# Splitting the K rows of three cross-attentions on GpSimd from an fp32 copy, with a four-slot ring of probabilities and an earlier fetch of the context

## The chip, the cores and the metric

The kernel runs on one NeuronCore of a Trainium2 chip. Its engines work side by side, each through its own instruction stream: TensorE (PE), VectorE (DVE), ScalarE (ACT), GpSimd (POOL) and SyncE (SP), which here issues nearly all DMAs. They wait for each other by semaphores. The metric is the device time of one execution in microseconds (us).

## The reference

A chain of four blocks updates x, of shape 16 batches x 56 tokens x 128. Block 0 attends from x to a context of 1500 rows per batch with one head of width 128, and sends the result through a router with three experts. Blocks 1, 2 and 3 each hold one cross-attention of 16 heads of width 8 to the same context of 1500 rows; blocks 2 and 3 also hold a self-attention over the 56 tokens and an MLP. The cross-attention, as block 1 has it:

```python
xq = _ada_ln(x_q, t_vec, Wss_q, bss_q)
xkv = _ada_ln(x_kv, t_vec, Wss_kv, bss_kv)
q = (xq @ Wq + bq).reshape(B, Lq, nh, dh)          # B=16, Lq=56, nh=16, dh=8
kv = (xkv @ Wkv + bkv).reshape(B, Lkv, 2, nh, dh)  # Lkv=1500
k = kv[:, :, 0]
v = kv[:, :, 1]
scores = jnp.einsum('bqhd,bkhd->bhqk', q, k) / jnp.sqrt(jnp.float32(dh))
attn = jax.nn.softmax(scores, axis=-1)
out = jnp.einsum('bhqk,bkhd->bqhd', attn, v).reshape(B, Lq, H)
return x_q + (out @ Wp + bp)
```

Block 2 normalises the context without modulation, block 3 takes it as it is.

## The kernel before, in words

The queries and keys of a cross-attention are carried as sums of two fp16 numbers, a high part (`k_hi`) and a low part (`k_lo`, what is left of the fp32 value). The score matmuls contract over 50 rows: 2 rows that carry the row maximum, then high and low parts of 16 dims stacked as rows. To get the parts of K into these rows, each third of a batch's keys (500 columns, t = 0, 1, 2) is written to DRAM (`k_out`, two DMAs, L407) and read back six times into `k_st` (`k_in`, six DMAs, L419). SP issues both, in a fixed order.

A cross-attention loops over the 16 batches (`pipeline`: two batches ahead of the loop, ten in it, four behind it). One pass, `attend(batch, following, behind, third)`, runs through 12 slots c, one for each chunk of 125 keys. In a slot PE computes the scores of `batch` (`scores`, L1153), two or three tiles that find the row maxima of the following batch (`unit`, L1101, 24 per batch, in a ring of three PSUM banks), in odd slots the product of probabilities and values for two earlier chunks (`values`, L1127), and one step of the preparation of the batch after that, `behind`. The table `SLOT_MISC` puts the nine steps in slots: T0, T1, T2 (transposes of the context, L1011) in slots 1 to 3, K0, K1, K2 (the K projection, L1016) in slots 4, 6 and 8, V0, V1 (L1022) in slots 9 and 10, and V2 in slot 0 of the next pass. All nine share one PSUM bank, so each step waits until the one before it has been read out.

ACT takes exponentials of the scores into a ring of six buffers (`probs`, `RING`, L795) and reads the steps out: for K it writes `k_hi` in fp16 (L725). DVE finds the maxima (L1552) and computes `k_lo` from the same PSUM bank and `k_hi` (`k_low`, L1460), behind the maxima of the slot after the step. PE's next step waits on both semaphores:

```python
if was == "K":
    pe.wait_ge(sem("k_hi_done"), NT * n + wt + 1)
    pe.wait_ge(sem("k_lo_done"), NT * n + wt + 1)
```

At the end of a pass a short chain joins the engines: DVE turns the maxima into two fp16 parts (L1564 to L1566), PE moves them to rows (L1112), DVE and ACT write them beside the queries (L1574, L782).

POOL normalises the context of batch b+3 in blocks 1 and 2 (`normalise`, 12 instructions, L585) and has nothing to do in the loop of block 3. SP issues, in each pass, the third K part of `following`, the queries (`q_st`, `q_mx`, L454), then `k_out` and `k_in` of `behind`, and last the load of the context of batch b+4 (L373), which waits until T2 of `behind` is done.

The first 17 of the preparation steps of a block (all of batch 0, all but V2 of batch 1) run earlier, beside the experts of block 0 or beside the first eight batches of a self-attention (`AHEAD`, `ahead`). In a self-attention POOL makes three copies for each batch (`self_copies`, L544 to L548).

## Time and profile before

| | |
|---|---|
| median of three runs | 2054.87 us (2048.06 to 2065.39) |
| the profiled execution | 2056.51 us, of which the span of the trace is 2054.7 us |
| busy share of the span | PE 80%, weight loads 50%, DVE 60%, ACT 49%, POOL 21% |
| mean granted TensorE clock | 0.892 of full speed |
| loops of the cross-attentions | about 410 to 800, 1005 to 1395 and 1610 to 2000 us |
| DMA | 166 MB, 81 GB/s over the span |

The busy shares are averages over stages with different limits. A busy PE also counts time in which matmuls overlap in its pipeline. In the chain of work that ended last, "issue" is time in which the engine waited for nothing that the profile shows.

### The profile page before, as it was taken

Reading aid. Unit: us, or ns where it says so; the run is one execution under the profiler, and the core shown is the slowest. Engines: PE = TensorE matmul, PEld = TensorE weight load, DVE = VectorE, ACT = ScalarE, POOL = GpSimd, SP = SyncE. Lnnn points to the kernel's source line nnn. Section 1 sums busy time; section 2 is a strip of 40 time slices with the busy share of each in tenths; the row PEclk is TensorE's granted clock in tenths of the full one; section 3 lists DMA queues with packets and bytes.
Section 4 is the critical chain, followed back from the end, with each engine's and each line's share of the span. In section 5 each row is a group of like instructions: output and inputs, shape, how many; then the busy total and the mean of one; then the engine's idle time right before and its main releaser. Section 6 shows DMA issues by size and latency. Waiting matters only on the chain.

```text
span 2054.7 us, 53923 instructions
## 1 busy us (share of the span) xinstructions
PE 1635.4 (80%) x20495; PEld 1030.7 (50%) x20495; DVE 1236.0 (60%) x2433; ACT 1004.1 (49%) x1911; POOL 422.9 (21%) x611
## 2 busy tenths in 40 slices
PE   4788777588887887787688888887785888888876
PEld 3465544255555555443355555555342455555554
DVE  5454443567775776364677777773364777777762
ACT  1243322166665666242366666663242466666662
POOL 7000133013331333135033333310131000000000
PEclk9798988599998998796699999996796799999997
DMA  5021122234443442040344444430040444444410
GB/s 174 26 77 64 45 44 62 55 82 112 112 110 94 113 102 73 1 103 3 72 112 113 111 109 111 110 98 14 0 102 11 92 116 117 114 114 112 106 43 9
DMA packets 178537, 166.32 MB, mean 81 GB/s; under 512 B 67551, under 2 KB 168098, under 8 KB 178402
## 3 DMA queue, kind: packets, MB, share of 16 engines
q1 hardware_dynamic: 176818, 163.35, 30.2%
q8 instruction: 97, 1.59, 0.4%
q10 hardware_dynamic: 1008, 1.05, 0.2%
q14 instruction: 38, 0.31, 0.0%
q0 software_dynamic: 576, 0.02, 0.0%
HBM read 114.46 MB, written 40.08 MB: 75 GB/s over the span
## 4 chain that ended last, share of the span: by engine, by line
PE 64%; issue 13%; DVE 10%; ACT 10%; DMA 1%; POOL 1%; ACTq 0%; DVEq 0%; SPq 0%; POOLq 0%
PE PS L1127 11%; PE PS L1022 8%; PE PS L1153 8%; PE PS L1016 8%; PE PS L862 6%; PE PS L1101 5%; PE PS L1011 3%; PE PS L941 3%; ACT q_parts L795 2%; DVE mx L1552 2%; PE PS L1227 2%; PE PS L959 2%; ACT v_sb L729 2%; ACT cxT L720 2%; PE PS L932 1%
## 5 line engine op out<-in xcount | busy, mean ns | idle before, releaser
L1552 DVE TENSOR_REDUCE mx<-PS 112x1 f32<-112x500 f32 x1152 | 718.4, 671 | 295.8 <-PE PS L1101 291.5
L795 ACT ACTIVATE q_parts<-PS 125x448 f32<-125x448 f32 x1152 | 562.2, 544 | 108.8 <-PE PS L1153 105.0
L585 POOL TENSOR_SCALAR cx<-cx,norm_b 125x128 f32<-125x128 f32 x384 | 303.5, 813 | 590.7 <-DMA cx<-in_ctx 488.2
L1153 PE MATMUL PS<-q_st,k_st 50*125 50x112 f16 x4608 | 263.1, 236 | 40.1 <-ACT q_parts L795 23.2
L1153 PEld LDWEIGHTS PS<-q_st,k_st 50*125 50x125 f16 x4608 | 186.4, 140 | 213.7 <-ACT q_parts L795 121.7
L1101 PE MATMUL PS<-k_st,q_mx 50*112 50x500 f16 x1152 | 262.5, 403 | 38.8 <-issue 24.2
L1127 PE MATMUL PS<-q_parts,v_sb 125*18 125x112 f32 x9216 | 291.4, 270 | 0.0
L1127 PEld LDWEIGHTS PS<-q_parts,v_sb 125*18 125x18 f32 x9216 | 218.4, 101 | 60.7 <-issue 52.1
L729 ACT ACTIVATE v_sb<-PS 125x512 f32<-125x512 f32 x144 | 87.1, 605 | 186.7 <-PE PS L1022 186.6
L725 ACT ACTIVATE k_hi<-PS,vec 128x500 f16<-128x500 f32 x144 | 97.5, 677 | 129.0 <-PE PS L1016 129.0
L1101 PEld LDWEIGHTS PS<-k_st,q_mx 50*112 50x112 f16 x1152 | 91.5, 133 | 74.5 <-issue 44.9
L1460 DVE SCALAR_TENSOR_TENSOR k_lo<-PS,vec,k_hi 128x500 f16<-128x500 f32 x144 | 104.8, 728 | 20.0 <-ACT k_hi L725 20.0
L1011 PE MATMUL PS<-ident,cx 125*128 125x125 f32 x576 | 97.1, 293 | 22.6 <-ACT cxT L717 11.8
L1011 PEld LDWEIGHTS PS<-ident,cx 125*128 125x128 f32 x576 | 62.6, 146 | 63.4 <-issue 26.3
L1022 PE MATMUL PS<-L_xcond_Wkv,cxT 128*125 128x128 f32 x384 | 61.1, 308 | 27.3 <-issue 22.6
L1022 PE MATMUL PS<-L_xcond_W_kvc,cxT 128*125 128x128 f32 x384 | 61.1, 308 | 25.0 <-issue 22.9
L1016 PE MATMUL PS<-cxT,L_xcond_Wkv 128*128 128x500 f32 x96 | 54.7, 653 | 30.8 <-issue 25.9
L813 ACT ACTIVATE A<-A 56x896 f32<-56x896 f32 x32 | 30.4, 949 | 92.4 <-DVE A L1661 92.4
L1022 PE MATMUL PS<-L_xcond_ca_vw,cxT 128*125 128x128 f32 x384 | 55.2, 287 | 25.3 <-issue 22.9
L782 ACT ACTIVATE q_st<-PS 2x448 f16<-2x448 f32 x48 | 25.7, 535 | 101.4 <-PE PS L1112 100.0
L1392 DVE TENSOR_REDUCE neg<-PS 56x1 f32<-56x1500 f32 x16 | 27.4, 1711 | 77.1 <-PE PS L941 77.1
L1022 PEld LDWEIGHTS PS<-L_xcond_Wkv,cxT 128*125 128x125 f32 x384 | 52.2, 209 | 42.2 <-issue 36.5
(266 smaller groups left out, 1994.1 us busy)
## 6 DMA issues: line engine op xcount, KB each, us to landing
k_st<-k_dram SPq DMA_DIRECT2D x864, 62.5 KB, 2.2
cx<-in_ctx SPq DMA_DIRECT2D x56, 750.0 KB
k_dram<-k_hi SPq DMA_DIRECT2D x144, 125.0 KB, 1.8
k_dram<-k_lo SPq DMA_DIRECT2D x144, 125.0 KB, 2.0
v_sb<-in_ctx SPq DMA_DIRECT2D x8, 750.0 KB
q_mx<-q_all SPq DMA_DIRECT2D x48, 99.8 KB
q_st<-q_all SPq DMA_DIRECT2D x48, 99.8 KB
q_all<-q_dram SPq DMA_DIRECT2D x18, 196.0 KB, 6.4
```

What stands on the lines that cost most here:

```text
L585: last = pool.tensor_scalar(cx[:, p, c, :], cx[:, p, c, :], norm_b[:, p, 0, c:c + 1], norm_b[:, p, 1, c:c + 1], ALU.subtract, ALU.mult)
L729: act.activation(v_sb[:, p, TC * t:TC * t + TC, :, 0:2 * DH], PS[0:KC, bank, :].rearrange("p (c r d) -> p c r d", c=TC, r=NP), ACT.Copy)\
L795: act.activation(probs[:, c % RING, u * HR:(u + 1) * HR], PS[0:KC, (2 * c + u) % SC_RING, 0:HR], ACT.Exp).then_inc(sem("exp_done"), 1)
L862: last = mm(dst[:, u, :], wt, r(u), start=(k == 0), stop=(k == len(rows) - 1))
L1011: last = pe.transpose(PS[:, bank, c * KC:(c + 1) * KC], cx[:, p, TC * t + c, :], ident[0:KC, 0:KC])
L1016: mm(PS[:, bank, 0:TK], cr["kw"], cxT[:, TK * t:TK * t + TK], start=True, stop=True)\
L1022: last = mm(PS[0:KC, bank, c * D:(c + 1) * D], cxT[:, k0:k0 + KC], cr["vw"], start=True, stop=True)
L1101: mm(PS[0:PW, MX_BANK + u % MX_RING, 0:TK], q_mx[64 * a:64 * a + ROWS, p, k, :], k_st[64 * a:64 * a + ROWS, p, k, TK * t:TK * t + TK], sta ...
L1127: last = mm(PS[32 * j:32 * j + VW, PV_BANK, k * PW:k * PW + PW], v_sb[:, p, c, r, :], probs[:, c % RING, r * PW:r * PW + PW], start=(c == ...
L1153: last = mm(PS[0:KC, (2 * c + a) % SC_RING, k * PW:k * PW + PW], k_st[64 * a:64 * a + ROWS, p, k, c * KC:(c + 1) * KC], q_st[64 * a:64 * a ...
L1460: dve.scalar_tensor_tensor(out=k_lo[:, cols], in0=PS[:, bank, 0:TK], scalar=cr["kb"], in1=k_hi[:, cols], op0=ALU.add, op1=ALU.subtract)\
L1552: dve.tensor_reduce(mx[:, r, t:t + 1], PS[0:PW, MX_BANK + u % MX_RING, 0:TK], AX.X, ALU.max)\
```

## The change

Four things change, and the work that is computed stays the same.

1. ACT writes the whole K tile in fp32 into a new buffer, `k_full` (two batches deep). POOL makes `k_hi` from it by a cast and `k_lo` by a subtraction (`split_keys`). DVE's `k_low` is gone everywhere.
2. PE's next step waits for ACT's copy alone (`k_full_done`).
3. The ring of probabilities has four buffers in place of six.
4. SP issues the load of batch b+4 ahead of the K parts of `behind`.

POOL's split of the first two batches of a block (`split_first`) stands behind `self_copies` of the whole self-attention.

```diff
--- before.py
+++ after.py
@@ -31,7 +31,7 @@
 QUAD = 4
 ROWS = 2 + 3 * 2 * DH
 VW = 2 * DH + 2
-RING = 6
+RING = 4
 UNITS = NP * NT
 
 
@@ -180,6 +180,7 @@
         mod_b = sb("mod_b", [128, 2, 2])
 
 
+        k_full = sb("k_full", [128, 2, S])
         k_hi = sb("k_hi", [128, S], F16)
         k_lo = sb("k_lo", [128, S], F16)
         k_st = sb("k_st", [128, 2, QUAD, S], F16)
@@ -481,13 +482,13 @@
                         q_scores(following)
                     if behind:
                         q_max(behind)
+                        if not (isinstance(b, int) and b + 4 >= B):
+                            load((b + 4, i + 2, p))
                         k_out(behind, 0)
                         k_in(behind, 0)
                         k_out(behind, 1)
                         k_in(behind, 1)
                         k_out(behind, 2)
-                        if not (isinstance(b, int) and b + 4 >= B):
-                            load((b + 4, i + 2, p))
 
                 pipeline(sp, first, attend)
 
@@ -557,6 +558,22 @@
                     for p in range(2):
                         copies((2 * i + p, i, p))
 
+            def split_keys(layer, batch, t):
+
+                b, i, p = batch
+                n = B * (layer - 1) + b
+                cols = slice(TK * t, TK * t + TK)
+                ge_known(pool, ("k_full_done", NT * n + t + 1), (f"k_out{t}", 32 * n))
+                pool.tensor_copy(k_hi[:, cols], k_full[:, p, cols]).then_inc(sem("k_hi_done"), 1)
+                ge_known(pool, ("k_hi_done", NT * n + t + 1))
+                pool.tensor_tensor(k_lo[:, cols], k_full[:, p, cols], k_hi[:, cols], ALU.subtract)\
+                    .then_inc(sem("k_lo_done"), 1)
+
+            def split_first(layer):
+                for b in range(2):
+                    for t in range(NT):
+                        split_keys(layer, (b, 0, b), t)
+
             def cross_copies(layer, rest):
                 cr = cross_of(layer)
                 n0 = B * cr["n"]
@@ -600,6 +617,9 @@
                     if third and cr["norm"] is not None:
                         copies(third)
                         normalise(third)
+                    if behind:
+                        for t in range(NT):
+                            split_keys(layer, behind, t)
 
                 def first():
                     if cr["norm"] is not None:
@@ -614,13 +634,16 @@
                 pool.wait_ge(sem("bn_done"), B)
                 for p in range(2):
                     pool.memset(v_sb[:, p, :, :, 2 * DH:VW], 1.0).then_inc(sem("v_ones"), 1)
+                split_first(1)
                 cross_copies(1, True)
             if layers > 2:
                 cross_copies(2, False)
                 self_copies(2)
+                split_first(2)
                 cross_copies(2, True)
             if layers > 3:
                 self_copies(3)
+                split_first(3)
                 cross_copies(3, True)
 
 
@@ -721,9 +744,9 @@
                     elif kind == "K":
                         act.wait_ge(sem("k_ready"), NT * n + t + 1)
 
-                        ge(act, f"k_out{t}", 32 * n)
-                        act.activation(k_hi[:, TK * t:TK * t + TK], PS[:, bank, 0:TK], ACT.Identity, bias=cr["kb"])\
-                           .then_inc(sem("k_hi_done"), 1)
+                        ge(act, "k_lo_done", NT * (n - 2) + t + 1)
+                        act.activation(k_full[:, p, TK * t:TK * t + TK], PS[:, bank, 0:TK], ACT.Identity, bias=cr["kb"])\
+                           .then_inc(sem("k_full_done"), 1)
                     else:
                         act.wait_ge(sem("v_ready"), NT * n + t + 1)
                         act.activation(v_sb[:, p, TC * t:TC * t + TC, :, 0:2 * DH],
@@ -997,8 +1020,7 @@
                     else:
                         was, wt = MISC[k - 1]
                         if was == "K":
-                            pe.wait_ge(sem("k_hi_done"), NT * n + wt + 1)
-                            pe.wait_ge(sem("k_lo_done"), NT * n + wt + 1)
+                            pe.wait_ge(sem("k_full_done"), NT * n + wt + 1)
                         else:
                             ge(pe, {"T": "cxT_done", "V": "v_done"}[was], NT * n + wt + 1)
                     if kind == "T":
@@ -1443,33 +1465,12 @@
                 l0_recip(b)
                 l0_evidence(b)
 
-            def preparation(layer):
-
-                cr = cross_of(layer)
-                n0 = B * cr["n"]
-
-                def k_low(batch, k, bank=MISC_BANK):
-                    kind, t = MISC[k]
-                    if kind != "K":
-                        return
-                    b, i, p = batch
-                    n = n0 + b
-                    dve.wait_ge(sem("k_hi_done"), NT * n + t + 1)
-                    ge(dve, f"k_out{t}", 32 * n)
-                    cols = slice(TK * t, TK * t + TK)
-                    dve.scalar_tensor_tensor(out=k_lo[:, cols], in0=PS[:, bank, 0:TK], scalar=cr["kb"],
-                                             in1=k_hi[:, cols], op0=ALU.add, op1=ALU.subtract)\
-                       .then_inc(sem("k_lo_done"), 1)
-
-                return k_low
-
             l0_batches(l0_first, l0_both, l0_last, dve)
             for k in range(2):
                 dve.wait_ge(sem("std_done"), k + 1)
                 dve.reciprocal(rstd_all[:, k, :, :], std_all[:, :, :]).then_inc(sem("rstd_done"), 1)
             dve.wait_ge(sem("evid_ready"), 1)
             dve.tensor_copy(halves(A[5]), pair(0)).then_inc(sem("evid_done"), 1)
-            k_low = preparation(1)
 
             for e in range(E):
                 dve.wait_ge(sem("router_ready"), e + 1)
...
@@ -1614,9 +1609,6 @@
                             finish((b - 1, None, 1 - p))
                         for t in tiles:
                             unit(following, t)
-                        of_next, k = SLOT_MISC.get(c - 1, (True, None))
-                        if behind and not of_next:
-                            k_low(behind, k)
                     if following:
                         shift_split(following)
                     if p == 0 and not start:
...
```

SP, one pass in the loop of block 1, before (DMA rows by out<-in; L454 are the queries, L407 and L419 the K parts, L373 the context of batch b+4):

```order
L454 DMA q_mx<-q_all 114x4x112
L278 ISA
L407 DMA k_dram<-k_hi 128x500
L407 DMA k_dram<-k_lo 128x500
...
L222 REGISTER_ALU
L373 ISA
L373 DMA cx<-in_ctx 125x1536
L278 REGISTER_ALU
L419 DMA k_st<-k_dram 16x4x500 x6
```

The same place in the changed kernel (its lines are one further down):

```order
L455 DMA q_mx<-q_all 114x4x112
L223 ISA
L374 ISA
L374 DMA cx<-in_ctx 125x1536
L279 ISA
L408 DMA k_dram<-k_hi 128x500
L408 DMA k_dram<-k_lo 128x500
L279 ISA
L420 DMA k_st<-k_dram 16x4x500 x6
```

The context load moved ahead of all three pairs of K writes of its pass, and ahead of the first two groups of six K reads; the third group stands at the start of the next pass in both.

POOL, one pass in the loop of block 1, in the changed kernel (before, the rows of L567 and L569 and the two L279 between them were not there):

```order
L586 COPY norm_b<-mean_all 125x12
L588 REGISTER_ALU
L588 COPY norm_b<-rstd_all 125x12
L223 REGISTER_ALU
L594 ISA
L594 COPY mod_b<-mod 128x2
L279 ISA
L602 TENSOR_SCALAR cx<-cx,norm_b 125x128 x12
L279 ISA
L567 CAST k_hi<-k_full 128x500
L569 TENSOR_TENSOR k_lo<-k_full,k_hi 128x500
...
```

The split of three tiles of `behind` follows the normalising of the batch after it, in POOL's own order.

DVE around K0 in the loop of block 1, before:

```order
L1552 TENSOR_REDUCE mx<-PS 112x1
L1457 ISA
L222 REGISTER_ALU
L1460 SCALAR_TENSOR_TENSOR k_lo<-PS,vec,k_hi 128x500
L1551 REGISTER_ALU
L1552 TENSOR_REDUCE mx<-PS 112x1
```

In the changed kernel the maxima follow each other without it, and nothing else moved on DVE.

## Rows read from the trace of the kernel before

**Rows 1.** The page, part 4: the chain that ended last, shares by engine.
```profile
PE 64%; issue 13%; DVE 10%; ACT 10%; DMA 1%; POOL 1%; ACTq 0%; DVEq 0%; SPq 0%; POOLq 0%
```

**Rows 2.** That chain in order of time, 500 to 560 us: start, us, what.
```profile
501.19 0.57 issue
...
505.19 0.86 issue
...
508.81 1.53 issue
```

**Rows 3.** The timeline, 500 to 545 us, all engines: start, us, engine, line, operation, out<-in.
```profile
500.94 0.73 DVE L1460 SCALAR_TENSOR_TENSOR k_lo<-PS,vec,k_hi 128x500 f16<-128x500 f32 x1
501.76 1.08 PE L1016 MATMUL PS<-cxT,L_xcond_Wkv 128*128 128x500 f32 x2 [0.57 <-issue]
...
502.88 0.68 ACT L725 ACTIVATE k_hi<-PS,vec 128x500 f16<-128x500 f32 x1 [0.89 <-PE PS L1016]
...
509.51 0.73 DVE L1460 SCALAR_TENSOR_TENSOR k_lo<-PS,vec,k_hi 128x500 f16<-128x500 f32 x1
...
515.35 0.31 SPq L373 DMA_DIRECT2D cx<-in_ctx  x1
...
526.14 0.68 ACT L725 ACTIVATE k_hi<-PS,vec 128x500 f16<-128x500 f32 x1 [0.41 <-PE PS L1016]
```

**Rows 4.** PE's waits in block 1's loop, 420 to 790 us: total us, times, longest.
```profile
PE PS L1022 <- issue: 22.6, 15, 1.5
PE PS L1016 <- issue: 20.0, 28, 0.9
```

**Rows 5.** The waits of the whole trace, same columns.
```profile
PE PS L1016 <- issue: 72.0, 91, 3.0
...
PE PS L1022 <- issue: 68.4, 45, 1.5
```

**Rows 6.** The page, part 5: busy us, mean ns; idle before, releaser.
```profile
L1552 DVE TENSOR_REDUCE mx<-PS 112x1 f32<-112x500 f32 x1152 | 718.4, 671 | 295.8 <-PE PS L1101 291.5
...
L1460 DVE SCALAR_TENSOR_TENSOR k_lo<-PS,vec,k_hi 128x500 f16<-128x500 f32 x144 | 104.8, 728 | 20.0 <-ACT k_hi L725 20.0
```

**Rows 7.** Busy us by engine in stretches: PE, PEld, DVE, ACT, POOL; clock, DMA share, GB/s.
```profile
517.10:543.67 26.57, 22.45 (x370) 15.05 (x371) 19.48 (x35) 17.31 (x34) 9.74 (x15) 1.00 0.44 113
...
1726.18:1752.38 26.20, 22.58 (x370) 15.05 (x371) 19.57 (x36) 16.67 (x35) 0.00 (x0) 1.00 0.44 113
```

**Rows 8.** POOL's groups by form: busy us, mean ns.
```profile
L548 POOL TENSOR_TENSOR q_parts<-A,mask 128x896 f32<-128x896 f32 x32 | 54.1, 1689 | 0.0
...
L545 POOL COPY A_first<-A 128x112 f32 x28 | 7.9, 282 | 0.0
L544 POOL COPY A_first<-A 128x56 f32 x28 | 6.5, 231 | 95.5 <-PE PS L1227 95.5
```

**Rows 9.** SP's timeline in block 3's loop, 1705 to 1765 us.
```profile
1726.18 0.35 SPq L407 DMA_DIRECT2D k_dram<-k_hi  x1
...
1728.76 2.66 SPq L419 DMA_DIRECT2D k_st<-k_dram  x6
...
1738.09 0.31 SPq L373 DMA_DIRECT2D cx<-in_ctx  x1
...
1743.32 3.02 SPq L454 DMA_DIRECT2D q_mx<-q_all  x1
```

**Rows 10.** POOL's timeline, 300 to 1700 us.
```profile
526.04 9.35 POOL L585 TENSOR_SCALAR cx<-cx,norm_b 125x128 f32<-125x128 f32 x12 [18.09 <-DMA cx<-in_ctx]
...
1555.44 1.69 POOL L548 TENSOR_TENSOR q_parts<-A,mask 128x896 f32<-128x896 f32 x1
```

**Rows 11.** SP's timeline between self- and cross-attention of block 3, 1380 to 1640 us.
```profile
1528.43 8.93 SPq L419 DMA_DIRECT2D k_st<-k_dram  x18
1584.04 0.81 SPq L441 DMA_DIRECT2D q_dram<-q_parts  x2
```

**Rows 12.** Line 1566: duration in ns min/median/max, first and last start.
```profile
L1566 DVE SCALAR_TENSOR_TENSOR msplit<-mneg,msplit x48: 170/171/341, 408.3 to 1987.9; 112x8 f16<-112x8 f32 x48
```

More of the change, by code:

```diff
@@ L1493, in _ @@
             for k in range(2 * E + 1):
-                if layers > 1:
-                    ahead(k_low, AHEAD[3 * k:3 * k + 1], DENSE_BANK)
                 dve.wait_ge(sem("hid_tanh"), k + 1)
@@ L1502, in _ @@
                                          op0=ALU.add, op1=ALU.mult).then_inc(sem("hid_done"), 1)
-                if layers > 1:
-                    ahead(k_low, AHEAD[3 * k + 1:3 * k + 3], DENSE_BANK)
                 if k == 1:
@@ L1544, in cross @@
                     last.then_inc(sem("q_split"), 1)
-                k_low = preparation(layer)
                 def unit(batch, u):
@@ L1641, in self_attention @@
                 s, _, bs, _, ob = SELF[layer]
-                k_low = preparation(layer)
                 dve.wait_ge(sem("self_lin"), 2 * s + 1)
@@ L1675, in both @@
                     front(n)
-                    ahead(k_low, beside[0:1], SELF_BANK)
                     back(b)
-                    ahead(k_low, beside[1:3], SELF_BANK)
                 batches(dve, front, both, back)
```

## The prediction, written before the changed kernel was timed

> **What bounds the kernel now.** I read the chain that ended last first. PE holds 64% of it, and 13% is "issue", time without a releaser in the profile [rows 1]. In order of time, most of this in the loops is three gaps per pass: 0.57 us ahead of K1, 0.86 us ahead of K2, 1.53 us ahead of V0 [rows 2]. Then the timeline: DVE's subtraction for K0 starts at 500.94 and takes 0.73, so it ends at 501.67; PE's K1 starts at 501.76, 0.09 later. For K2 it ends at 510.24 and V0 starts at 510.34, 0.1 later [rows 2, 3]. ACT's copy of K1 was over by 503.56, while PE was still in the scores and maxima of its slot [rows 3]. So these gaps are PE's wait for `k_lo`: DVE is free to take it up only behind the maxima of the next slot. They total 2.96 us a pass. Rows 4 repeat this over one loop: 20.0 us in 28 gaps (14 passes, two each) and about 1.5 us each ahead of V0. DVE itself is not the bound. It is busy 19.5 of 26.2 to 26.6 us per pass, ACT 16.7 to 17.3, POOL 9.7, PE 22.5 [rows 7]. It is the order on DVE that costs.
>
> **The change part by part.**
>
> *PE's waits in the loops.* `behind` exists in 14 passes of each of three blocks, 42 in all. 42 x 2.96 = 124.3 us. ACT's K copy (0.68 us) starts 0.04 us after the projection ends and precedes ACT's exponentials of the slot, so it is over before PE wants the bank in slots 4 to 9. Does something else wait there at once? I moved the pass of rows 3 up by the gaps. DVE then has the 8 tiles of slots 7 to 9 in about 5.0 us of PE's work; at 671 ns each [rows 6] that is 5.4 us, less where they follow each other, with 2.2 us of subtractions gone (728 ns x 3 [rows 6]). The three-bank ring lets DVE lag by three tiles, and V0, 1.1 us without a maximum, lets it catch up. ACT has 17.3 us of work in a pass of then 23.6 [rows 7]. I take the whole 124.3; the bounds are none of it (0) and all.
>
> *The steps ahead of the loops.* Beside the dense stage and the self-attentions the projection follows more closely. Of the whole trace's 91 and 45 gaps, 84 and 42 lie in loops; 7 and 3 remain, with 72.0 - 60.0 = 12 us and 68.4 - 42 x 1.53 = 4 us [rows 4, 5]. ACT's copy stays in these, DVE's 0.73 + 0.09 goes: 10 x 0.82 = 8 us at most, 0 if the softmax chain of these stages hides it. I take 5.
>
> *POOL's two instructions per tile.* The trace has no cast or subtraction of 500 elements on POOL. Copies of 56 and 112 elements take 231 and 282 ns, 0.91 ns an element, so 0.64 us for 500 (fp16 output, no row: up to the 0.73 of DVE and more). The two-input one takes 1689 ns for 896 [rows 8]: 0.94 us by proportion, 1.69 us at most. So 1.6 to 2.7 us a tile with semaphores 1.9, 5.7 us a pass. With the normalising (9.74 [rows 7]) POOL is at 15.4 of 23.6 us in blocks 1 and 2, at 5.7 in block 3. Its split of `behind` stands behind the normalising of the next batch, and that behind the context load. That load is now issued at slot 3 of the pass before and lands some 10.7 us later at worst (515.35 to POOL's start at 526.04 [rows 3, 10]). POOL then starts normalising when it has split K2, at about 18 us of a pass, and ends 9.35 us later [rows 10], some 4.5 us into the next; K0's copy ends 9.7 us into a pass (526.82, of the pass that starts at 517.10 [rows 3, 7]). Covered, with 5 us to spare. Without the earlier load the normalising would end about when K0 is ready.
>
> *SP.* The number of DMAs stays. SP's chain of a pass runs from `k_out` of K0 through three landings and three groups of reads to the end of `q_mx`: 1726.18 to 1746.34, 20.2 us with the load inside [rows 9]. K0's parts leave 1.1 us later than before (1.9 against 0.73 plus waiting for the maxima, which about evens out). The load goes some 4.5 us ahead of them: T2 is one slot before K0's projection, which starts 1.1 us ahead of ACT's copy at 526.14 [rows 3], and the parts are there at 528.7. SP has been idle in that time. The pass shrinks to 23.2, so SP has 3.0 us left. The reads of K0 are issued by 16.9 us of a pass (9.7 + 1.9, then 2.58 to the first read and 2.66 for the six [rows 9]) and are wanted at its end, those of K1 and K2 only at units 8 and 16 of the next. I take 0.
>
> *Ring of four.* ACT waits for the values of chunk c-4 ahead of chunk c. In PE's order they stand ahead of the scores of chunk c in every slot, the first ones of a pass too, and ACT needs those scores anyway. 0 us; nothing covers it, it cannot end last.
>
> *Between the stages.* The K parts of batches 0 and 1 used to leave during the self-attention; now six tiles are split behind POOL's last copy. In block 3 this copy ends at 1557.13 [rows 10]. Three tiles (5.7) and a pair of writes (0.8), load (0.3), 18 reads (8.9 [rows 11]), three pairs of writes (2.3), load (0.3), 18 reads (8.9): 1584.3. SP should write the queries at 1584.04 [rows 11], so it is just late, later if reads wait for their writes, and the queries share the DMA engines with what is in flight: 0 to +6, I take +3. In block 2 the norm lies between, which makes it 0.
>
> *The shared port.* The last of the three small DVE operations that split the maxima reads two SBUF operands: 171 ns typically, 341 ns once [rows 12]. POOL now works nearly always in blocks 1 and 2, so it may more often have to wait for one instruction, up to 0.78 us for one of the twelve of the normalising (9.35 / 12 [rows 10]). 28 passes x 0 to 0.78 is 0 to 22 us; the median of 171 beside a POOL busy for a third of the pass is nearer to nothing, and I take 3.
> The Trainium skill (SBUF — State Buffer, Who interferes with whom) says that DVE and GpSimd share one pair of ports under an exclusive lock, that a DVE instruction with two SBUF inputs is fully blocked by a reading GpSimd instruction, and that a tensor_reduce is never. By it the sum would hold these 3 us and up to 22; were the rule void it would be 3 us lower. The single 341 ns agrees; nothing in this trace settles it.
>
> *Sum.* 2056.5 - 124.3 - 5 + 3 + 3 = 1933 us against the profiled execution, which lies 1.6 us above the median.
>
> **The rivals.**
>
> *Another engine takes the gaps (maxima or exponentials).* If DVE's maxima still lag where PE now comes sooner, half of the V0 gap returns: 0.8 x 42 = 34 us, 1967. For: DVE's 5.4 against PE's 5.0 us above. Against: the rest of its pass is loose, 17.3 of 23.6 us.
>
> *The load pushes the K rows.* If K0's writes land only with the whole load, 10.7 us after its issue, they land 6.2 us after theirs in place of 2: SP's chain becomes 24.4 us and sets the pass. 1.2 x 42 = 50 us of the gain are lost: 1984. Against: 10.7 us was with six reads and the queries just behind the load [rows 3, 9], which are now not there.
> The Trainium skill (DMA: Bandwidth & Descriptors, Queues, rings and completion order) says that descriptors of one ring are consumed in order on each DMA engine, so writes issued behind a load queue behind its bytes. By it this rival, not the forecast, would hold if the load were that long; no row shows the load alone.
>
> *Slower.* The same mechanism at more than one landing. SP has 6.0 us up to the old 26.2 us pass; from there on every pass is longer than before. Two landings late by 4.2 us each give 28.6 us, 2.4 x 42 = 101 us more: 2157. For it: `q_mx` takes SP 3.02 us to issue when a load and six reads are in flight [rows 9]. Against: by K1 the load has had over 9 us.
>
> *It does not do what it says.* If the gaps were the sequencer's own time and the 0.1 us a coincidence, only DVE is relieved: about 2050, within 1%. Against: it would be the same coincidence each time.
>
> **How the numbers follow.** Forecast 0.62 (1905 to 1955), another engine takes part 0.15 (1955 to 1975), the load pushes the K rows 0.12 (1975 to 2000), no effect 0.05, slower 0.03, better than 1905 0.03 (more overlap than I count). The time is that of the likeliest: 1933 us. The range 1905 to 1985 takes the first two and half of the third, about 0.83. One per cent, about 20 us, is what a measurement of this kernel tells from nothing. Faster by over 1%: 0.62 + 0.15 + 0.12 + 0.03 = 0.92; within 0.04; slower 0.04.
>
> **What would show it.** In the profile after: no gap of 0.57, 0.86 and 1.53 us ahead of K1, K2 and V0, and a pass of about 23.2 us; waits of PE for maxima (first rival) or of PE for `k_st` reads or queries, with SP without idle time (second and third); POOL's cast and subtraction at 1.6 to 2.7 us a tile; SP's first query write in block 3 directly behind the last K reads. The prediction is wrong if POOL needs over 3.5 us a tile, since its pass would then exceed 20 us and K2's parts would be late, or if the pass stays above 25 us with the gaps gone.

## The result, and the profile after

| kernel | median | runs | lowest to highest |
|---|---|---|---|
| before | 2059.76 us | 4 | 2048.06 to 2065.39 |
| changed | 1986.99 us | 4 | 1983.16 to 1990.89 |

The changed kernel takes 0.9654 of the time before (95% interval 0.96 to 0.9708). That is 73 us faster, where 122 were forecast (1933 against the 2054.87 known then), and 2 us outside the range. The profiled execution took 1983.74 us with a span of 1981.9, against 2054.7 before.

The chain that ended last comes first again. These are its shares by engine and by line, on the page of the changed kernel:

```profile
PE 44%; DMA 16%; SPq 10%; issue 9%; DVE 9%; ACT 6%; POOL 6%; DVEq 0%; POOLq 0%; ACTq 0%
```

PE held 64% of it before, and DMA 1% [rows 1]. Now DMA and SP's queue hold 26% together. In order of time, 1739 to 1771 us, in block 3's loop (start, us, what):

```profile
1739.40 6.39 DMA k_dram<-k_lo
...
1749.10 1.87 DMA k_dram<-k_lo
...
1754.26 1.95 DMA k_dram<-k_lo
...
1762.43 8.15 DMA k_dram<-k_lo
```

The chain runs through SP from one write of K parts to the next. The waits for K0 are 6.4 and 8.2 us long, those for K1 and K2 1.9 and 2.0: the write that stands behind the context load is the long one. SP's own timeline shows where the load is (1690 to 1765 us of the changed kernel; start, us, queue, line, what):

```profile
1712.08 0.38 SPq L374 DMA_DIRECT2D cx<-in_ctx  x1
1715.94 0.35 SPq L408 DMA_DIRECT2D k_dram<-k_hi  x1
...
1721.31 2.68 SPq L420 DMA_DIRECT2D k_st<-k_dram  x6
...
1736.67 0.51 SPq L374 DMA_DIRECT2D cx<-in_ctx  x1
1739.00 0.35 SPq L408 DMA_DIRECT2D k_dram<-k_hi  x1
...
1745.86 2.67 SPq L420 DMA_DIRECT2D k_st<-k_dram  x6
...
1760.26 0.78 SPq L455 DMA_DIRECT2D q_mx<-q_all  x1
1761.35 0.46 SPq L374 DMA_DIRECT2D cx<-in_ctx  x1
```

Read it from load to load. K0's reads, which wait for K0's writes to land, start 9.2 us after the load both times (1712.08 to 1721.31, 1736.67 to 1745.86), although the writes left 3.9 us after it in one pass and 2.3 us in the other. Over the twelve loads in this loop the reads start 9.0 to 9.9 us after the load, with K0's writes 0.6 to 4.6 us behind it. So K0 lands a fixed time after the load's issue, not after its own. The load's own landing is in no row of this loop; where POOL waits for a load (e2 below, 559.86 to 569.84) it is 10.0 us, with K reads behind it. From these reads to the next load SP is in its fixed order for 15.5 us (1745.86 to 1761.35). 9.2 + 15.5 = 24.7 us is the distance of the loads, and SP has no slack in it.

SP's waits in this loop, 1540 to 1930 us, in the changed kernel (total us, times, longest):

```profile
SPq L223 <- DMA k_dram<-k_lo: 116.4, 42, 7.8
```

In the kernel before, 1640 to 1940 us, in the same loop (same columns; these rows were not shown ahead):

```profile
SPq L222 <- DVE k_lo L1460: 58.2, 12, 6.3
SPq L222 <- DMA k_dram<-k_lo: 50.4, 35, 3.4
```

Where SP used to wait for DVE (idle time that cost nothing), it now waits for landings: 8.3 us a pass (116.4 / 14), where three of 1.5 us would be 4.5. PE pays for it in front of the maxima, which read `k_st` (PE's timeline in the changed kernel, 1590 to 1610 us, idle time in brackets):

```profile
1599.05 0.77 PE L1123 MATMUL PS<-k_st,q_mx 50*112 50x500 f16 x2 [4.21 <-DMA k_st<-k_dram]
1599.76 2.07 PE L1044 MATMUL PS<-L_xcond_ca_vw,cxT 128*125 128x128 f32 x8
```

After a wait of 4.2 us the V step takes 2.07 us in place of 1.14. The granted clock of the stretches ahead of the wait, behind it and after that says why (stretch, us, PE busy, granted clock, DMA share, GB/s):

```profile
1585.00:1595.00 10.00, 9.58 (x201) 1.00 0.36 121
1599.50:1608.00 8.50, 8.50 (x76) 0.50 0.42 104
1609.00:1620.00 11.00, 10.91 (x173) 1.00 0.36 116
```

It stood at 2.4 GHz ahead of the wait, was at 1.2 GHz behind it although PE was busy all the time, and stood at 2.4 GHz again in the last row. Over whole loops this shows in the mean. First the kernel before, blocks 1 and 3, from first to last scores, then the changed one (same columns):

```profile
409.90:827.40 417.50, 346.70 (x5674) 0.95 0.38 99
...
1610.50:2007.20 396.70, 337.99 (x5676) 0.97 0.38 99
```
```profile
392.40:783.50 391.10, 352.19 (x5674) 0.92 0.38 105
...
1547.00:1933.10 386.10, 355.11 (x5674) 0.92 0.37 102
```

The gaps of [rows 2] and [rows 4] are gone. K1, K2 and V0 of one pass in the changed kernel have no idle time ahead of them:

```profile
1738.11 1.11 PE L1038 MATMUL PS<-cxT,L_xcond_ca_kw 128*128 128x500 f32 x2
...
1741.49 1.11 PE L1038 MATMUL PS<-cxT,L_xcond_ca_kw 128*128 128x500 f32 x2
...
1744.21 1.14 PE L1044 MATMUL PS<-L_xcond_ca_vw,cxT 128*125 128x128 f32 x8
```

POOL's new work, on the page, part 5 (busy us, mean ns; idle before), answers to the estimate from [rows 8]:

```profile
L567 POOL CAST k_hi<-k_full 128x500 f16<-128x500 f32 x144 | 87.4, 607 | 698.0 <-ACT k_full L748 352.3
...
L569 POOL TENSOR_TENSOR k_lo<-k_full,k_hi 128x500 f16<-128x500 f32 x144 | 163.9, 1138 | 21.1 <-POOL k_hi L567 4.5
```

Where the 72.8 us of the span came from, by the first and the last scores of each loop. One such row for each kernel (duration min/median/max in ns, first to last start), first before, then changed:

```profile
L1153 PE MATMUL PS<-q_st,k_st x1536: 217/218/355, 409.9 to 827.4; 50*125 50x112 f16 x192
```
```profile
L1175 PE MATMUL PS<-q_st,k_st x1536: 217/218/353, 392.4 to 783.5; 50*125 50x112 f16 x192
```

| part of the span | before | changed | difference | forecast |
|---|---|---|---|---|
| up to block 1's loop | 409.9 | 392.4 | -17.5 | -5 |
| the loops of blocks 1, 2, 3 | 417.5, 407.9, 396.7 | 391.1, 379.1, 386.1 | -65.8 | -124.3 + 3 (port) |
| between blocks 1 and 2 | 178.2 | 178.2 | 0.0 | 0 |
| between blocks 2 and 3 | 197.0 | 206.2 | +9.2 | +3 |
| behind block 3's loop | 47.5 | 48.8 | +1.3 | 0 |

Each stretch is from one profiled execution. The first one varies: it ends at 392.4 to 398.3 us in the kernels below that have the change, and at 409.9 and 407.5 us in the kernel before and in e12, so the change is worth 9 to 17 us there.

### The profile page after: what moved, and what is told of

Its sections match the earlier page's. It is cut to its first block, busy times and chain, and to the rows that moved or that the text cites. A ratio compares the mean times of both kernels' runs of the same rounds, so it can differ in the third digit from the quotient of the medians.

```text
span 1981.9 us, 54153 instructions
## 1 busy us (share of the span) xinstructions
PE 1648.7 (83%) x20495; PEld 1047.8 (53%) x20495; DVE 1151.3 (58%) x2289; ACT 1006.1 (51%) x1911; POOL 676.4 (34%) x899
## 4 chain that ended last, share of the span: by engine, by line
PE 44%; DMA 16%; SPq 10%; issue 9%; DVE 9%; ACT 6%; POOL 6%; DVEq 0%; POOLq 0%; ACTq 0%
DMA k_dram<-k_lo 12%; SPq L420 7%; PE PS L1149 6%; PE PS L885 5%; PE PS L1175 4%; PE PS L1044 4%; POOL cx L602 4%; PE PS L1038 4%; DMA k_st<-k_dram 3%; PE PS L1123 3%; PE PS L964 3%; PE PS L1033 3%; DVE mx L1547 2%; PE PS L1249 2%; PE PS L982 2%
## 5 line engine op out<-in xcount | busy, mean ns | idle before, releaser
L1123 PE MATMUL PS<-k_st,q_mx 50*112 50x500 f16 x1152 | 270.4, 416 | 93.7 <-DMA k_st<-k_dram 42.1
L567 POOL CAST k_hi<-k_full 128x500 f16<-128x500 f32 x144 | 87.4, 607 | 698.0 <-ACT k_full L748 352.3
L1175 PE MATMUL PS<-q_st,k_st 50*125 50x112 f16 x4608 | 268.3, 239 | 39.4 <-ACT q_parts L818 23.2
L569 POOL TENSOR_TENSOR k_lo<-k_full,k_hi 128x500 f16<-128x500 f32 x144 | 163.9, 1138 | 21.1 <-POOL k_hi L567 4.5
L1123 PEld LDWEIGHTS PS<-k_st,q_mx 50*112 50x112 f16 x1152 | 99.5, 137 | 135.3 <-issue 99.8
L748 ACT ACTIVATE k_full<-PS,vec 128x500 f32<-128x500 f32 x144 | 97.4, 676 | 60.7 <-PE PS L1038 60.7
L1033 PE MATMUL PS<-ident,cx 125*128 125x125 f32 x576 | 108.9, 320 | 18.3 <-ACT cxT L740 10.4
L1033 PEld LDWEIGHTS PS<-ident,cx 125*128 125x128 f32 x576 | 70.6, 160 | 63.9 <-issue 27.5
L743 ACT ACTIVATE cxT<-PS 128x500 f32<-128x500 f32 x96 | 56.9, 593 | 39.6 <-PE PS L1033 39.6
L1649 DVE TENSOR_REDUCE s_mx<-PS 56x16 f32<-56x896 f32 x32 | 34.6, 1082 | 60.4 <-PE PS L1249 60.4
L1249 PE MATMUL PS<-q_parts,A_first 128*56 128x448 f32 x128 | 68.8, 625 | 0.0
```

Source lines behind the costliest of these rows:

```text
L569: pool.tensor_tensor(k_lo[:, cols], k_full[:, p, cols], k_hi[:, cols], ALU.subtract)\
L748: act.activation(k_full[:, p, TK * t:TK * t + TK], PS[:, bank, 0:TK], ACT.Identity, bias=cr["kb"])\
L1033: last = pe.transpose(PS[:, bank, c * KC:(c + 1) * KC], cx[:, p, TC * t + c, :], ident[0:KC, 0:KC])
L1123: mm(PS[0:PW, MX_BANK + u % MX_RING, 0:TK], q_mx[64 * a:64 * a + ROWS, p, k, :], k_st[64 * a:64 * a + ROWS, p, k, TK * t:TK * t + TK], sta ...
L1175: last = mm(PS[0:KC, (2 * c + a) % SC_RING, k * PW:k * PW + PW], k_st[64 * a:64 * a + ROWS, p, k, c * KC:(c + 1) * KC], q_st[64 * a:64 * a ...
L1249: last = mm(PS[0:T, 2 * p + u, 0:HR], q_b[:, p, :], km_b[:, p, NP * u:NP * u + NP, :].rearrange("p h t -> p (h t)"), start=True, stop=True)
```

## The experiments

Each ratio is to the kernel before, timed beside the run (medians of 2055 to 2061 us).

Theory 1: the changed kernel has lost PE's gaps, and the context load, issued just ahead of K0's writes, has made SP's chain of writes, landings and reads the bound of the pass. Rivals: DVE or ACT took the gaps over; POOL is late with the parts; the shorter ring makes ACT late; and, of theory 1 itself, that the load delays K0 only because both are in one queue.

**A small load (e1).** The loads in the loops bring one of twelve chunks of the context; the later batches work on old rows, so the attended context is another one. All instructions stay.

```diff
-                            load((b + 4, i + 2, p))
+                            load((b + 4, i + 2, p), 1)
```

> The changed kernel, but in the passes of the three loops the load of the context of batch b+4 brings one of its 12 chunks (62.5 KB in place of 750 KB), so the context of later batches is wrong. Theory 1 (the load stands in SP's ring ahead of the K parts, K0's writes land only with it, and SP's chain of 24.5 us sets the pass): K0's writes land after about 2 us, the pass falls to 23.2 to 23.6 us and the time to about 1935 to 1945 us. Theory 2 (all DMA engines together are too slow for the pass, wherever the load stands) says the same here. Theory 3 (PE's maxima, DVE or a lower granted clock set the pass, DMAs do not): 1980 to 1990 us, as the changed kernel.

Measured: 1897.00 us (1892.03 to 1910.37), ratio 0.927 (0.9218 to 0.9322), 90 us under the changed kernel. The loops are 364.1, 353.2 and 351.8 us. SP's timeline in block 3:

```profile
1615.80 0.35 SPq L409 DMA_DIRECT2D k_dram<-k_hi  x1
...
1618.13 2.67 SPq L421 DMA_DIRECT2D k_st<-k_dram  x6
...
1632.40 0.78 SPq L456 DMA_DIRECT2D q_mx<-q_all  x1
...
1637.81 0.35 SPq L409 DMA_DIRECT2D k_dram<-k_hi  x1
```

K0's reads start 1.5 us after its writes have been issued. The chain from K0's writes to the end of `q_mx` is 17.4 us (1615.80 to 1633.18), the pass 22.0 (1615.80 to 1637.81), and SP is idle for the rest of it. DVE, ACT, POOL and the ring are as in the changed kernel, so none of them holds it at 1987 us. The theory stands, and the price is larger than I had written (1935 to 1945 us). This run alone does not tell the order of SP's chain from the mere number of bytes in flight; e8 does.

**The load at its old place (e2), and with it POOL's split ahead of the normalising (e10).** e2 is the changed kernel with this; e10 has it too, and in POOL's pass the three `split_keys` stand ahead of `normalise`:

```diff
-                        if not (isinstance(b, int) and b + 4 >= B):
-                            load((b + 4, i + 2, p))
                         k_out(behind, 0)
...
                         k_out(behind, 2)
+                        if not (isinstance(b, int) and b + 4 >= B):
+                            load((b + 4, i + 2, p))
```

> The changed kernel with the load back at its old place behind the K parts. Theory 1: in the loop of block 3, where POOL normalises nothing, the pass falls to about 23.5 us (loop some 15 us shorter than 386 us). In blocks 1 and 2 POOL's split of K0 stands behind a normalising that now waits for the late load: K0 is split some 8 us later, the pass grows to 26 us or more, and the whole is slower than the changed kernel, about 2020 to 2080 us. Theory 2: block 3's loop stays at 386 us, since the bytes are the same. Theory 3: nothing moves anywhere, 1987 us.

> The kernel with the load at its old place, with POOL's split of a pass now ahead of its normalising. If the 33 us passes of blocks 1 and 2 come from K0's split standing behind a normalising that waits for the late load, they fall: K0 is split when it is there, the normalising runs from about 18 us of a pass to 5 us into the next, and T0 waits for it some 3 us: passes of 25 to 27 us in blocks 1 and 2, 23.3 us in block 3, in all 1985 to 2030 us. If the load's bytes at that place are the cause, they stay near 33 us and the time near 2187 us.

Measured: e2 2187.15 us (2182.69 to 2190.23), ratio 1.0656 (1.0609 to 1.0703); e10 2019.78 us (2009.70 to 2029.95), ratio 0.9827 (0.9776 to 0.9879). In e2 a pass takes about 33 us in blocks 1 and 2 and, after the first two, about 23.3 in block 3, which has no normalising. POOL's timeline of e2 in block 1:

```profile
569.84 9.36 POOL L602 TENSOR_SCALAR cx<-cx,norm_b 125x128 f32<-125x128 f32 x12 [17.52 <-DMA cx<-in_ctx]
579.14 0.61 POOL L567 CAST k_hi<-k_full 128x500 f16<-128x500 f32 x1
```

The pass is a circle: POOL sits idle 17.5 us until the load lands, normalises for 9.4, splits the three tiles in one go, and only then can SP write them, read them and issue the next load. e10 cuts the circle at POOL and most of its passes in blocks 1 and 2 are 25 to 28 us, as written for it. So without the earlier load the change would have been slower by 6.6%. The block that has nothing to normalise shows what the old place is worth by itself: its pass is shorter than in the changed kernel (24.5). The direction of e2 was as expected, the size was not: I had not counted that all three tiles are late together.

**The load on ACT's queue (e3).** ACT issues it, behind T2:

```diff
-                            load((b + 4, i + 2, p))
...
                             misc(following if of_next else behind, k)
+                            if k == 2 and not of_next and not (isinstance(b, int) and b + 4 >= B):
+                                act.dma_start(cx[:, p, :, :], ctx[bass.ds(b + 4, 1)]
```

> The changed kernel with the loop's context loads issued on ACT's own DMA queue, right behind ACT's copy of T2 (the same time as before, the same bytes). Theory 1: another queue lets K0's writes pass the load, they land in 2 to 4 us, the pass is 23.2 to 24 us, the time 1940 to 1962 us. Theory 2: the same DMA engines have the same bytes to move in the same stretch, 1980 to 1990 us. Theory 3: 1987 us.

Measured: 1983.82 us (1976.91 to 1992.08), ratio 0.9681 (0.9627 to 0.9734), the changed kernel's time. ACT's load and SP's timeline in block 3:

```profile
1708.62 0.27 ACTq L814 DMA_DIRECT2D cx<-in_ctx  x1
```
```profile
1710.04 3.21 SPq L455 DMA_DIRECT2D q_mx<-q_all  x1
1713.48 3.50 SPq L408 DMA_DIRECT2D k_dram<-k_hi  x1
1717.10 0.36 SPq L408 DMA_DIRECT2D k_dram<-k_lo  x1
1719.59 2.67 SPq L420 DMA_DIRECT2D k_st<-k_dram  x6
```

K0 now lands within 2.1 to 5.0 us of its issue, but the two DMAs that SP issues while the load is under way take 3.2 and 3.5 us to issue, in place of 0.8 and 0.35. K0's reads start 11.0 us after the load (8.9 to 13.0 over all loops), hardly sooner than before. In other passes the load catches K2's reads instead. Two passes earlier ACT issues it at 1655.71, while SP issues these reads. Their landing, from the chain that ended last, and then PE's wait for it, from PE's timeline:

```profile
1657.28 8.57 DMA k_st<-k_dram
```
```profile
1665.98 0.66 PE L1124 MATMUL PS<-k_st,q_mx 50*112 50x500 f16 x1 [4.99 <-DMA k_st<-k_dram]
```

The usual landing of such a read is 2.2 us. The theory that one queue is the cause falls; what stands is that the load delays SP's small DMAs by several us whoever issues it, and only the victim and the form change. The time lies where I had written it for another theory, that all bytes together bind the pass (1980 to 1990 us); e8 decides against that one. The Trainium skill (DMA: Bandwidth & Descriptors, Queues, rings and completion order) says that each DMA engine takes turns between the queues that it has work for. K0's shorter landing agrees; the 3.5 us of issue is not in that rule, and nothing here shows what SP stands still for. It is not tied to a second queue: `q_mx` took 3.02 us to issue in the kernel before, behind a load in SP's own queue [rows 9].

**Writes ahead of reads (e8), and this with the small load (e13).** e8 is the changed kernel with SP's order turned so that no landing is waited for directly behind its write (e13 works on another context, as e1 does):

```diff
                         k_out(behind, 0)
-                        k_in(behind, 0)
                         k_out(behind, 1)
-                        k_in(behind, 1)
+                        k_in(behind, 0)
                         k_out(behind, 2)
+                        k_in(behind, 1)
```

> The changed kernel with SP's order in a pass: load, write K0, write K1, read K0, write K2, read K1. If the serial chain of SP (three times write, wait for the landing, read; the first landing behind the load) sets the pass, K1's and K2's landings now lie beside other work: the chain falls from 24.5 us by 2 x 1.6 us and a part of the first wait, under the 22.3 us which the pass takes with a small load, and the time to 1905 to 1935 us. If instead the bytes of load and K parts together set the pass, in whatever order, the time stays at 1980 to 1990 us.

> The reordered kernel with one chunk of 12 loaded in the loops (the context of later batches is wrong). If the order of K writes and reads has taken the whole price of the load off the pass, it stays within 1% of the reordered kernel's 1896 us and of the 1897 us of the small load in the old order. If the load's bytes still cost something, it is 1870 to 1885 us.

Measured: e8 1895.61 us (1893.88 to 1897.59), ratio 0.9229 (0.918 to 0.9277); e13 1895.43 us (1891.19 to 1900.30), ratio 0.9223 (0.9145 to 0.9301). SP's timeline of e8 in block 3:

```profile
1659.34 0.30 SPq L374 DMA_DIRECT2D cx<-in_ctx  x1
1663.81 0.35 SPq L408 DMA_DIRECT2D k_dram<-k_hi  x1
...
1666.90 0.32 SPq L408 DMA_DIRECT2D k_dram<-k_hi  x1
...
1668.30 2.68 SPq L420 DMA_DIRECT2D k_st<-k_dram  x6
...
1679.35 0.78 SPq L455 DMA_DIRECT2D q_mx<-q_all  x1
1681.34 0.30 SPq L374 DMA_DIRECT2D cx<-in_ctx  x1
```

K0's reads still start 9.0 us after the load, but K1's writes go out in the meantime. From load to `q_mx` the chain is 20.8 us (1659.34 to 1680.13), and the next load is issued 22.0 us after this one: SP has time left again. The load is still there in full, with the same bytes, and taking it away as well (e13) gains nothing. So the order of write, wait and read was the whole price of the load, and the bytes together do not bind the pass. e8 came out 9 us under the range written for it. The whole loops of blocks 1 and 3 (same columns as above):

```profile
395.10:752.90 357.80, 334.05 (x5676) 0.98 0.41 115
...
1491.60:1845.60 354.00, 336.80 (x5674) 0.97 0.40 111
```

**The gaps brought back (e11).** e8, and in the loops PE's next step waits for the low part too, now POOL's:

```diff
                             pe.wait_ge(sem("k_full_done"), NT * n + wt + 1)
+                            if bank == MISC_BANK:
+                                pe.wait_ge(sem("k_lo_done"), NT * n + wt + 1)
```

> The reordered kernel (load, write K0, write K1, read K0, write K2, read K1), but in the loops PE's step after a K projection waits for the low part as well, as in the kernel before; POOL makes it 1.8 us after ACT's copy. If PE's wait for the low part is what the change took away, gaps come back ahead of K1, K2 and V0, about 0.6, 0.6 and 0.9 us by POOL's times, some 2 us a pass, 42 passes: 84 us slower than 1896 us, 1960 to 2000 us. If the gain came from relieving DVE, it stays at 1896 us.

Measured: 2007.89 us (2003.99 to 2012.74), ratio 0.9758 (0.9675 to 0.9842): 112 us slower than e8, and 8 us above the range written for it, since the three gaps are 2.5 us a pass and not 2. PE and POOL in block 3:

```profile
1712.07 1.08 PE L1040 MATMUL PS<-cxT,L_xcond_ca_kw 128*128 128x500 f32 x2 [0.84 <-issue]
...
1719.93 1.11 PE L1046 MATMUL PS<-L_xcond_ca_vw,cxT 128*125 128x128 f32 x8 [1.13 <-issue]
```

```profile
1710.84 1.13 POOL L569 TENSOR_TENSOR k_lo<-k_full,k_hi 128x500 f16<-128x500 f32 x1
```

POOL's subtraction ends at 1711.97 and PE starts at 1712.07. The profile calls these 0.84 us "issue" although the kernel was given that very wait: an "issue" gap can be a wait on a semaphore. This shows that the reading of [rows 2, 3] is right. It also shows the rival "it does not do what it says" to be wrong.

**Parts of the change, in the kernel before (e4, e12).** e4: `RING = 4` and the load ahead of the K parts. e12: SP's order of e8 alone.

> The kernel before with only two parts of the change: the ring of four and the load ahead of the K parts; DVE still makes the low part. Theory 1: the gaps ahead of K1, K2 and V0 stay and the pass with them; SP's chain of 24.5 us still fits under 26.2 us: 2045 to 2070 us, no change. If the ring of four made ACT wait, it would be slower than before by several us per block. Theory 3: no change either.

> The kernel before with nothing but the new order of SP's K writes and reads. In it SP's chain of 20.2 us has 6 us to spare under the 26.2 us pass, and PE's waits for the low part set the pass: no change, 2045 to 2065 us. If SP's chain was already a bound beside the gaps, it is faster by tens of us.

Measured: e4 2059.20 us (10 runs), ratio 1.0018 (0.9983 to 1.0053); e12 2060.00 us (10 runs), ratio 1.0005 (0.9955 to 1.0055). Neither does anything. While PE waits for DVE 3 us a pass, SP has the time to spare, so its chain has no price there. The same edit of SP's order is worth 91 us once PE's waits are gone. The ring was tried together with the load only, never by itself, and a ring of six was not tried in the changed kernel.

**The first six tiles split beside the self-attention (e6), and both improvements together (e9).** POOL splits batches 0 and 1 between `self_copies` of batches 5 to 11; e9 adds e8's order.

```diff
+            SPLITS = {5: [(0, 0)], 6: [(0, 1)], 7: [(0, 2)], 10: [(1, 0)], 11: [(1, 1), (1, 2)]}
...
+                for n in range(2, 12):
+                    copies((n, n // 2, n % 2))
+                    for b, t in SPLITS.get(n, []):
+                        split_keys(layer, (b, 0, b), t)
+                with pool.Fori(6, B // 2) as i:
```

> The changed kernel, but POOL splits the six K tiles of batches 0 and 1 beside the self-attentions (one or two tiles behind the copies of batches 5, 6, 7, 10 and 11) and not behind the last copy. If SP's late K parts cost time ahead of block 3's loop (the stretch from block 2's last to block 3's first scores grew from 197.0 to 206.2 us), that stretch comes back to about 197 us and block 2's stays at 178 us: some 9 us less, 1978 us. Rival: the stretch is longer for another reason (DMA contention of the query writes, clock), and nothing moves: 1987 us.

> The two edits before together: if they are independent, their gains add up, 1895 to 1925 us, some 9 us below the reordered writes alone.

Measured: e6 1981.33 us (1975.42 to 1984.04), ratio 0.9647 (0.9596 to 0.9698); e9 1886.67 us (1883.49 to 1895.53), ratio 0.9177 (0.9127 to 0.9226). The stretch between the loops of blocks 2 and 3 shows the effect better than the time: 206.2 us in the changed kernel and 197.5 in e6 (197.0 before), 207.1 in e8 and 194.2 in e9. In all runs with the split behind the last copy it is 203.9 to 208.6. e9 has the lowest median of all, 8.2% under the kernel before and 5% under the changed one; its interval and that of e8 overlap, so the last 9 us are not shown by the time alone.

## Why the prediction was wrong

**The step that failed is "SP", with its "I take 0".** I counted SP's chain from K0's writes to `q_mx` as 20.2 us with the load inside [rows 9], saw 3.0 us left in a pass of 23.2, and held that the load goes into idle time ahead of the chain. The runs show that K0's reads start about 9.2 us after the load is issued, so the load is a link of the chain and not something ahead of it. Counted from load to load it is 9.2 + 15.5 = 24.7 us. That is over 23.2, and no lead of the load over K0's writes changes it, since the load itself stands behind `q_mx` in the same order. This is the rival "the load pushes the K rows": 24.4 us a pass and 1984 us were written there, 24.5 in the mean of block 3's later passes and 1983.74 in the profiled execution came. Its chance of 0.12 was too low. The argument against it, that the 10.7 us of [rows 3, 10] had reads and queries behind the load, would have made the load shorter, and it was: 9.2. But 24.4 against 23.2 left room for only 1.2 us of error.

That the rival's 1984 us was met almost exactly is partly luck. It took 124 us of gain and 50 us of loss. The runs show 155 us of gain in the loops (e8 against before) and 89 us lost again (changed against e8), and the two errors cancel. Its chain was also made up otherwise: the 20.2 us of [rows 9] hold a `q_mx` that took 3.02 us to issue behind the load, where it takes about 0.8 now, and leave out the time from the load to K0's writes.

The Trainium skill (DMA: Bandwidth & Descriptors, Queues, rings and completion order), cited in the prediction for writes behind a load in one ring, gave the right result here. e3 shows that its reason is not the whole one: with the load in another ring the time is the same.

**PE's waits in the loops: right, and even too small.** The gaps went, and e11 pays 112 us for having them again. In e8, where SP is out of the way, the loops are 357.8, 355.4 and 354.0 us: 59.7, 52.5 and 42.7 us under those of before, 154.9 in sum, against 124.3 forecast. PE's busy time, its idle time and the granted clock over each whole loop (us busy + us idle, clock), from the view of the rows above:

| loop | before | changed | e8 | e11 |
|---|---|---|---|---|
| block 1 | 346.7 + 70.8, 0.95 | 352.2 + 38.9, 0.92 | 334.1 + 23.7, 0.98 | 341.5 + 64.5, 0.96 |
| block 2 | 349.0 + 58.9, 0.94 | 347.1 + 32.0, 0.94 | 337.8 + 17.7, 0.97 | 339.4 + 52.5, 0.97 |
| block 3 | 338.0 + 58.7, 0.97 | 355.1 + 31.0, 0.92 | 336.8 + 17.2, 0.97 | 338.3 + 52.4, 0.97 |
| sum | 1033.7 + 188.4 | 1054.4 + 101.9 | 1008.6 + 58.6 | 1019.2 + 169.3 |

From before to e8 the idle time falls by 129.8 us. Of this 5.4 us are one gap ahead of the scores of block 1 that e8 does not have; the rest is the 124.3 forecast. The busy time falls by 25.1 us more, nearly all of it in blocks 1 and 2, where the granted clock was lower. The matmuls are the same. This second gain was not in my sum.

**What of it was lost again.** The changed kernel's loops are 1156.3 us against e8's 1067.2. Of these 89 us, 43 are idle time (101.9 against 58.6) and 46 are busy time (1054.4 against 1008.6): the same matmuls at a lower granted clock. Few long waits cost more here than many short ones. e11 has 67 us more idle time than the changed kernel, in gaps of 1.2 us at most ahead of its K and V steps, and yet 35 us less busy time; the changed kernel waits for `k_st` up to 4.9 us at once.

**DVE and ACT: right.** With SP out of the way no rival engine took the gaps: PE waits 0.4 us for maxima in each loop of e8, and e1 and e8 came out under the forecast's 1933 us.

**POOL: right.** 607 and 1138 ns against estimates of 640 and at least 940; with the semaphore between them about 1.85 us a tile. That it depends on the earlier load was said, and e2 shows it with 200 us.

**Ring of four: as forecast.** e4 shows no cost of it in the kernel before, and e8 runs with it at 1896 us.

**Steps ahead of the loops: too small.** -17.5 us against -5, or 9 to 17 with the spread of this stretch. It lies ahead of block 1's loop, where single gaps were longer than the 0.82 us that I allowed for each (one of 2.98 us beside the dense matmuls before, 1.73 at that place now; one of 1.98 us, none now). I had capped the gain at DVE's own time and forgotten that DVE came to the subtraction late there too. No run takes this part alone.

**Between the stages: right place, too small.** +9.2 us against +3, and e6 gives back 8.7. The changed kernel's SP timeline shows why:

```profile
1506.76 9.03 SPq L420 DMA_DIRECT2D k_st<-k_dram  x18
1515.97 0.82 SPq L442 DMA_DIRECT2D q_dram<-q_parts  x2
1522.55 2.68 SPq L448 DMA_DIRECT2D q_all<-q_dram  x6
```

The query write stands directly behind the last K reads, as foretold, and then lands 5.8 us after it was issued (1516.79 to 1522.55), where before the reads followed 1.2 us behind it. My +3 had named the transfers in flight without a price for them. It also left out a wait ahead of this: SP stands 4.8 us in front of batch 1's K writes (1498.26 to 1503.09), because `k_out` waits until the reads of batch 0's parts have landed, and the two batches now follow each other at once.

**The shared port: nothing to be seen, in place of 3.** The row that answers to [rows 12]:

```profile
L1561 DVE SCALAR_TENSOR_TENSOR msplit<-mneg,msplit x48: 170/171/384, 390.8 to 1913.0; 112x8 f16<-112x8 f32 x48
```

The median stays at 171 ns beside a POOL that is busy for 34% of the span instead of 21%. By the Trainium skill (SBUF — State Buffer, Who interferes with whom) the two-input instruction can be blocked by a reading POOL. The trace agrees: the three of the 48 that took over 0.25 us (at 646.62, 1032.42 and 1229.59) and the one of 341 ns before (806.54) all start during a normalising of POOL. But they are too rare to cost anything.

## What to carry to other kernels

When a wait is taken off the bounding engine, the next bound may be a chain of issues and landings on the DMA-issuing engine that looks idle in every share. Count it once all the way round, from one DMA to the same DMA of the next pass, with the landing of each transfer that something waits for, the large one included, and compare it with the pass as it will be. If a write, a wait for its landing and a read follow each other on one queue, put the next write ahead of the wait: here that costs nothing before, and is worth 91 us after.

## What the hardware showed that I had not expected

- Two small writes issued 2.3 or 3.9 us behind a load of 125 x 1536 fp32 values land about 9.2 us after that load's issue. Behind a load of a twelfth they land in 1.5 us (e1).
- With the load on another engine's queue the small writes land sooner, but the small DMAs that SP issues meanwhile take 3.2 and 3.5 us to issue in place of 0.8 and 0.35 (e3), and reads of K2 that went out beside it took up to 8.6 us to land in place of 2.2.
- A wait of PE of 4.2 us is followed by 8.5 us at a granted clock of 0.50. Over the whole loops the granted clock is 0.97 to 0.98 in e8, and 0.92 to 0.94 in the changed kernel with the same matmuls.
